# In steps with two lane 0 tile jobs, the first job's gate goes between the scans and the C product

## The reference, cut to what matters

```python
# layer 0's mixer: a selective state space, for 16 states n
dA  = exp(dt[..., None] * A)
dBx = (dt * xc)[..., None] * Bm[:, :, None, :]
def step(h, inp):
    dA_t, dBx_t, C_t = inp
    h = dA_t * h + dBx_t
    return h, einsum('bdn,bn->bd', h, C_t)
# both layers' feed-forward: softmax over 8 experts, the top 2, and a shared expert
y = sum_e comb[:, e] * ((silu(x @ w1[e]) * (x @ w3[e])) @ w2[e])
x = x + mixer(norm(x)) * silu(ffn(norm(x)))
```

## Time and profile before

| | |
|---|---|
| median of the runs | 1165.83 us (1163.33 to 1166.81) |
| the profiled execution | 1170.12 us |
| its span | 1168.3 us |
| busy: PE, DVE | 912.0 us (78%), 955.0 us (82%) |
| busy: ACT, POOL | 608.9 us (52%), 604.2 us (52%) |
| mean granted TensorE clock | 0.897 |

### The profile page before, as it was taken

How to read it: one execution, slowest core, us unless ns; L and a number is a source line. 1 busy time by engine, 2 the same in 40 slices (tenths; PEclk the granted TensorE clock), 3 DMA queues, 4 the chain that set the end, 5 groups by cost and what they waited for, 6 DMA issues and landing times.

```text
span 1168.3 us, 16985 instructions
## 1 busy us (share of the span) xinstructions
PE 912.0 (78%) x4556; PEld 644.6 (55%) x4556; DVE 955.0 (82%) x1804; ACT 608.9 (52%) x1593; POOL 604.2 (52%) x422
## 2 busy tenths in 40 slices
PE   3467678867767869886888889887876788889888
PEld 1344466545545645564655566565554566656555
DVE  3697889898889898897989987999669886987445
ACT  2444545564547554654657555665445455555233
POOL 1238226648526535683347752584776547324540
PEclk9976899997788898897999989998978898888999
DMA  9954244457334434563545633474645466344201
GB/s 279 295 112 132 74 103 115 119 125 192 91 93 115 124 88 121 145 162 103 126 93 140 160 96 104 120 183 116 163 126 109 90 134 157 92 114 111 82 10 37
DMA packets 168650, 144.71 MB, mean 124 GB/s; under 512 B 15680, under 2 KB 135536, under 8 KB 168560
## 3 DMA queue, kind: packets, MB, share of 16 engines
q10 hardware_dynamic: 39776, 67.47, 26.3%
q1 hardware_dynamic: 121104, 60.43, 18.2%
q0 software_dynamic: 7680, 15.74, 4.4%
HBM read 106.88 MB, written 36.70 MB: 123 GB/s over the span
## 4 chain that ended last, share of the span: by engine, by line
PE 36%; DVE 31%; issue 14%; ACT 8%; POOL 5%; DMA 3%; ACTq 1%; another core or an unknown queue 1%; DVEq 0%; SPq 0%; POOLq 0%
DVE pA L1399 11%; PE pM L981 6%; PE pH L887 4%; PE pM L971 4%; DVE hj L1435 4%; POOL dBx L790 3%; PE pG L943 3%; PE p L946 3%; PE pU L944 3%; DVE hj L1447 2%; PE pG L946 2%; DVE hc L1407 2%; DMA bcb<-bc_rows 2%; PE pH L959 1%; POOL rows_in L732 1%
## 5 line engine op out<-in xcount | busy, mean ns | idle before, releaser
L790 POOL TENSOR_TENSOR dBx<-dtx,bcb 128x1024 f32<-128x1024 f32 (+1 forms) x144 | 304.6, 2115 | 409.3 <-DVE pA L1399 380.9
L887 PE MATMUL pH<-const,hc 128*128 128x128 f32 x1024 | 162.1, 305 | 44.3 <-DVE hc L1407 40.3
L1399 DVE TENSOR_TENSOR_SCAN pA<-pA,carry,dBx 128x512 f32<-128x512 f32 (+1 forms) x160 | 162.8, 1063 | 29.7 <-ACT pA L1001 20.8
L1001 ACT ACTIVATE pA<-dt,am 128x512 f32<-128x512 f32 (+1 forms) x288 | 173.9, 639 | 15.4 <-DVE hc L1407 7.8
L1399 DVE TENSOR_TENSOR_SCAN pA<-pA,dBx 128x512 f32<-128x512 f32 x128 | 149.8, 1216 | 30.4 <-ACT pA L1001 14.3
L887 PEld LDWEIGHTS pH<-const,hc 128*128 128x128 f32 x1024 | 128.5, 157 | 65.7 <-DVE hc L1407 48.4
L1407 DVE TENSOR_TENSOR hc<-pA,bcb 128x1024 f32<-128x1024 f32 (+1 forms) x144 | 159.2, 1106 | 5.0
L971 PE MATMUL pM<-const,hj 128*128 128x128 f32 (+3 forms) x636 | 129.7, 301 | 36.2 <-DVE hj L1447 10.1
L732 POOL DMA_INDIRECT rows_in<-xn,slots x120 | 127.7, 1064 | 30.1 <-issue 27.5
L1181 ACT ACTIVATE yj<-pM 128x128 f32<-128x128 f32 x236 | 65.3, 277 | 139.7 <-PE pM L981 124.6
L971 PEld LDWEIGHTS pM<-const,hj 128*128 128x128 f32 (+3 forms) x636 | 73.2, 140 | 109.1 <-issue 81.5
(11 more groups left out here) (205 smaller groups left out, 1534.0 us busy)
## 6 DMA issues: line engine op xcount, KB each, us to landing
bcb<-bc_rows ACTq DMA_DIRECT2D x112, 512.0 KB
rows_out<-yj SPq DMA_DIRECT2D x236, 64.0 KB
xg<-rows_in SPq DMA_DIRECT2D x176, 64.0 KB
bcb<-bc_rows ACTq DMA_DIRECT2D x32, 256.0 KB
rows_in<-gy SPq DMA_DIRECT2D x8, 512.0 KB, 8.8
mixed<-s_st SPq DMA_DIRECT2D x12, 256.0 KB
so<-rows_out SPq DMA_DIRECT2D x6, 512.0 KB
sr<-mixed SPq DMA_DIRECT2D x6, 512.0 KB
```

What stands on the lines that cost most here:

```text
L790: pool.tensor_tensor(dBx[:, N % 2, :, 0:t1 - t0], dtx[q % 2][:, :, t0:t1], row, ALU.mult).then_inc(dBx_ready, 1)
L887: last = mm(pH[:, half, c * DI + k * P:c * DI + (k + 1) * P], hc[:, N % 2, k, t * P:(t + 1) * P], ident, is_transpose=True, start=(n == 0 ...
L1001: A(pA[:, k, 0:t1 - t0], dt[q % 2][:, k, t0:t1], ACT.Exp, scale=am[:, k, n:n + 1]).then_inc(decay_ready, 1)
L1399: dve.tensor_tensor_scan(pA[:, k, 0:w], pA[:, k, 0:w], dBx[:, N % 2, k, 0:w], carry[:, k, N % NS:N % NS + 1] if N in carry_after else 0.0, ...
```

## The change

The C product becomes an item of its own, `hc`, and ACT's `carry`, decays and load of the next B and C rows go with it. In steps with one lane 0 job `hc` stands right behind `scan`, so that nothing moves. The first of the two last pieces of the diff is ACT's (`carry`, decays, load of rows), the second DVE's (the C product). In the 28 steps with two, the slot `c` (gate of the step's first job, `up` of the second) stands between `scan` and `hc`; the flip of slot `c` is held until behind `hc`, and lane 1's slot comes last.

```diff
-WITH_SECOND = "a scan b c hflip".split()
-WITH_ONE = "a scan b hflip".split()
-LAST_SCAN = "a scan hflip b".split()
+WITH_SECOND = "a scan c hc C b hflip".split()
+WITH_ONE = "a scan hc b hflip".split()
+LAST_SCAN = "a scan hc hflip b".split()
...
+            elif what == "hc":
+                if live:
+                    plan.append(("hc", step))
...
-                if what.upper() in order and (what == "b" or running[0] is None or lanes[0][running[0]][0] == 1) and len(plan) > before_slot and plan[-1][0] == "flip":
+                if what.upper() in order and (what in ("b", "c") or running[0] is None or lanes[0][running[0]][0] == 1) and len(plan) > before_slot and plan[-1][0] == "flip":
...
-                elif kind == "scan":
+                elif kind == "hc":
                     N, = a
                     q, t0, t1 = SEGS[N // NS]
                     if N in carry_no:
...
+                elif kind == "hc":
+                    N, = a
+                    w = SEGS[N // NS][2] - SEGS[N // NS][1]
                     dve.wait_ge(h_ready, 2 * N + 2)
```

## The result

The changed kernel takes 1178.02 us in the median of 13 runs (1167.90 to 1181.22), the kernel before 1167.57 us in 13 runs beside it (1162.86 to 1173.00). The ratio is 1.0067 with a 95% interval of 1.0042 to 1.0092: slower by 7.8 us (4.9 to 10.7). The forecast was slower by 5.9 us. As a time it was 1171.7 us with a range of 1161 to 1179, worked out from a kernel before at 1165.83 us; that kernel's median in the 13 runs is 1.7 us higher. The profiled execution took 1180.96 us, its span is 1179.2 us and its granted clock 0.90, so 10.9 us over the span before.

The account below looks back on a forecast made before the run. DVE, 82% busy, was taken as the bound: its instructions in order plus the holes between. Terms of +9.2 and −3.3 us gave +5.9 on 1165.83, about 1171.7 us, range 1161 to 1179.

Parts of the forecast that it names:

- term 1: Two-job steps: the second job's gate and `up` come earlier, closing holes before its gate; −3.3 us in sum.
- term 2: Two-job steps: the first job's gate loses the C product and lane 1's gate as cover for late tanhs; +9.2 us.
- the steps counted at nothing: Steps 2, 16, 18, 28, 32, 48, 52, 64, 80, 92 (extras fill the hole) and 72, 84: no gain expected.
- steps 12, 56, 88, 76, 4 and 36: First gates with late tanhs: +0.8, +1.8, +1.8, +1.3, and +1.2 each in 4 and 36.
- step 60: First gate +1.8 us, counted 0 because the scans of steps 63 and 64 wait 0.75 and 1.45 us for POOL.
- The small ones: Steps 20, 44, 68, 96, 100, tanh or copy 0.4 to 0.65 us late: 2.2 us in all, half taken.
- step 14: Second job earlier: gain of 0.8 us from a hole of 2.4, as a wait for the decays takes over.
- step 40: Second job earlier: gain of 0.6 us from a hole of 2.3, by the same walk as step 24.
- step 24: Second job earlier, no extras: scan at 3.95 us after the previous scan's end, not 4.84; gain of 0.9 us.
- TensorE's tail: Rival: in 12 steps with lane 1, its flip waits 0.7 us for `pM`, delaying the next tanh; 8.4 us more, 1180; chance 0.13.
- Steps 72 and 84: Lane 1 active: DVE alone would win 1.3 us each, but the next step's ranks or decays take it back; counted nothing.
- the faster rival: Rival: later holes swallow most of term 2 while term 1 stays; about 1160 us, far end 1154; chance 0.13.

Follow-up runs that it names:

- experiment 3: New order only in steps 2, 16, 18, 28, 32, 48, 52, 64, 72, 80, 84 and 92, against the kernel before: 1168.32 us, ratio 1.0011.
- experiment 4: In the 12 steps with lane 1, second lane 0 slot ahead of lane 1's but behind the C product, against the kernel before: 1172.57 us, ratio 1.0039.
- Experiment 10: New order in steps 14, 22, 24 and 40 only, second job's flip not held behind the decays, against the kernel before: 1161.35 us, ratio 1.0042.
- experiment 9: New order only in steps 2, 14, 16, 18, 22, 28, 52, 80, 84 and 92, against the kernel before: 1151.02 us against 1156.58, ratio 0.9954.
- experiment 5: Old order everywhere, four added ACT copies at the head of eleven quiet steps, against the kernel before: 1154.83 us, ratio 1.0005.

## Why the prediction was right, and where it was not

**Direction and size: right.** Slower by 5.9 us was forecast, and 7.8 (4.9 to 10.7) was measured. The total is better than its parts. By the table and the small steps below, term 1 is −1.8 us for the −3.3 forecast, term 2 is +8.3 for +9.2, and the steps counted at nothing gave 1.0 (the seven of experiment 3). That is +5.5, so the errors of the parts nearly cancel, which was luck; the 2.3 us from there to the measured 7.8 are within the interval.

**Term 2, the first job's gate loses its cover: right.** It was named for steps 12, 56, 88, 76, 4 and 36 at 8.1 us; the table has 7.1 for these six, and 6.5 was timed with the new order in them and step 60 alone. The walk "start of the gate after the scans' end, less the holes already there" was good to 0.1 us in steps 4, 12 and 88, and in 56 too when equally late tanhs are compared (+1.8; the mean's +0.6 sets a tanh that came mostly at 2.5 against one that came mostly at 4.5). It was too high in 36 (+0.6 for +1.2). In 76 (+2.4 for +1.3) the size was missed for a reason that no walk through one trace can see. The table load of before began at 616.40, 0.48 us before the scan, and in the changed kernel it began 1.09 us after it. In three of seven traces in the old order it is that late too, and the step takes 9.2 us and not 8.16. Whether the new order makes it late is open: both traces of the new order that have the logarithm in this step have it late, and so does that of experiment 4. The small ones, counted at 1.1, came to 0.3 in step 44 and 0.5 in step 68, and none in 20, 96 and 100 (10.25 and 10.61 for 10.39).

**Step 60, counted at nothing: right in size, for another reason.** The tanh came 0.90 us after the scans' end, not 2.56 later, so little was there to absorb. That the waits for POOL at steps 63 and 64 would shrink was wrong, and with it the announced sign that the stretch would end in shorter ones. The same rows in the changed kernel, DVE:

```profile
510.56 2.47 DVE L1402 TENSOR_TENSOR_SCAN pA<-pA,carry,dBx 128x512 f32<-128x512 f32 x2 [2.11 <-POOL dBx L793]
...
516.74 2.35 DVE L1402 TENSOR_TENSOR_SCAN pA<-pA,dBx 128x512 f32<-128x512 f32 x2 [1.47 <-POOL dBx L793]
```

They are 2.11 and 1.47 us for 0.75 and 1.45.

**Term 1, the second job earlier: the sum was wrong, −3.3 for −1.8.** The second waits named are gone or small as said (0.40 us in step 14, 0.61 in step 40), but the sizes are not those of the walk. In step 14 I had the copy and the decays hold the scan. They held it 0.29 us, and the step won 1.8. In step 24 I had the first gate start with the scans' end. In the changed kernel, DVE:

```profile
222.06 0.52 DVE L1440 SCALAR_TENSOR_TENSOR hj<-tj,pG 128x352 f32<-128x352 f32 x1 [0.63 <-ACT tj L1169]
222.73 0.52 DVE L1452 TENSOR_TENSOR hj<-hj,pU 128x352 f32<-128x352 f32 x1 [0.15 <-ACT xgT L1162]
```

Both halves of the gate wait, 0.78 us in all, so `up` of the second job starts 0.8 us later than in my walk and of the 0.9 us a third is left. The copy to `xgT` was in the trace of before too, 0.5 us behind the scans' end, hidden under the C product: I had walked past it. The largest miss is step 40: its −0.6 nearly stands (−0.5), but step 41 lost 1.8 behind it. A part of the cause is one that I had named myself as the rival "TensorE's tail" and looked for only in the steps with lane 1: the copies of the second flip behind the decays keep `pM`. Experiment 10 takes the hold away and the loss goes, with the low clock of step 41. In the steps with lane 1, where I had put it, nothing like 8.4 us shows (steps 64, 68 and 92: 0, +0.5 and −0.2).

**Steps 72 and 84.** Step 72 wins 1.5 us and the next step gives it all back in the wait for the ranks, in each of the three traces of the new order, as forecast. Step 84 takes 8.3 to 8.5 us in the new order and 8.5 to 9.8 in the old. Some of that is kept: it was one of the steps of experiment 9. I had counted nothing.

**The signs that were announced.** The waits for the tanh rose (+7.8 us in steps 0 to 101), the first gates wait behind the scans in 4, 12, 36, 56, 60, 76 and 88 (0.90 us in step 60, up to 4.76 in 56), and DVE's busy time is 951.8 for 955.0: right. Scans that wait for decays in place of the second tanh: only 0.29 us in step 14 and 0.30 in step 40, none in steps 22 and 24, so that bound came out too strict. Two sums of the prediction are slightly off: the holes before the second job's gates come to 11.2 us and those before the first job's to 7.5 when read again, not 11.7 and 7.1. Of the sum nothing hangs on them, only the far end of the faster rival.

**The rule weighed.** The Trainium skill (Perfetto Trace Analysis, Optimization Strategy) would start earlier what the gaps of the engine being optimised wait for. In step 14 that is worth 1.8 us. In step 88 the same order costs 1.75, since an earlier producer was bought with an earlier consumer of something else. Experiment 9 is the rule applied where the traces show a gain. On table loads the rows of step 76 say what the earlier trace rows said: the load ends at 625.70 and the tanh starts at 625.72, with no drain between.

## What to carry to other kernels

When an order moves a waiting instruction up on the engine that bounds the kernel, price two things in each place: the hole behind it that closes, and its own start after the point it is moved to, less the holes that were there. Where the second is positive the engine idles first and does the work that had covered the wait afterwards, as in steps 56, 76 and 88, and the price ends at the length of that work; a list of places beats one rule for all (1.0067 for all, 0.9954 for ten chosen). And follow a copy that is pushed behind others on its engine to the next user of its PSUM bank, two or three products further on, before calling the push free. And compare stretches of two traces only where what they wait for came equally late.

## What the runs showed of the hardware that was not expected

The granted clock of one and the same stretch varies between executions and moves steps that nobody touched. The windows over the same work of the kernel before (steps 4 and 58; from the left: length in us, busy time of the engines, granted clock, DMA share, GB/s):

```profile
69.10:80.10 11.00, 5.88 (x32) 3.81 (x30) 9.89 (x24) 4.94 (x13) 2.35 (x1) 0.93 0.63 111
...
466.00:477.00 11.00, 9.40 (x41) 6.34 (x40) 8.96 (x21) 6.87 (x17) 5.11 (x4) 0.73 0.46 118
```

and of the changed one:

```profile
68.40:82.10 13.70, 8.96 (x36) 5.57 (x34) 9.76 (x24) 5.02 (x13) 2.34 (x1) 0.75 0.39 89
...
466.00:479.00 13.00, 11.40 (x40) 7.51 (x38) 8.24 (x21) 6.09 (x13) 5.24 (x4) 0.61 0.33 75
```

In step 4 PE is busy for 8.96 us at a clock of 0.75, where it was 5.88 us at 0.93 (with 36 matmuls in the window for 32). That stretch is 2.7 us longer. About 1.1 of it is the new order; the rest is a tanh that came 1.6 us later. Two traces in the old order have it at 14.3 us, with a clock of 0.62, where the others have about 11.0, with 0.92 to 1.00. So one pair of traces can be wrong by 3 us in a single step. Step 56 shows the same: with a clock of 1.00 over the step the tanh comes 2.5 to 2.8 us after the scans' end, with 0.86 to 0.89 it comes 4.5 to 4.9 us after it. Other steps repeat to 0.01 us in every trace (step 88: 12.73 and 12.74 in the old order, 14.49 and 14.50 in the new one). And the chips differ: the kernel before takes 1167.5 us on one and 1156.6 on another, more than the change is worth. The difference doesn't lie in the steps that were changed. From the first scan to that of step 102 the trace of before has 773.5 us and that of experiment 5, on a faster chip and in the same order, 773.6; behind it they have 351.1 and 332.5.
